# Experts of a routed feed-forward layer worked off by halves of 512 slots

## The reference, cut to what matters

```python
x = x + 0.5 * ffn(layernorm(x))     # first part
x = x + attention(layernorm(x))     # 16 heads, causal, with positions from a running sum
x = x + 0.5 * ffn(layernorm(x))     # second part, the same weights
```

```python
probs = softmax(xf @ gate_w.T)                   # [8192, 8]
scores_sel = route(probs)                        # 0 where a token isn't kept
h = gelu(einsum('nd,efd->enf', xf, w1))          # exact gelu
y_e = einsum('enf,edf->end', h, w2)
y = einsum('ne,end->nd', scores_sel, y_e)
```

## Time and profile before

| | |
|---|---|
| median of 3 runs | 2959.88 us (2959.29 to 2960.41) |
| profiled execution, its time | 2933.87 us |
| its span, first to last instruction | 2931.7 us |
| busy: PE / PEld / DVE / ACT / POOL | 84% / 65% / 58% / 57% / 34% of the span |
| instructions | 104032 |
| mean granted TensorE clock | 0.918 of full speed |
| DMA | 207.26 MB, mean 71 GB/s |

### The profile page before, as it was taken

How to read it: one execution, slowest core, us unless ns; L and a number is a source line. 1 busy time by engine, 2 the same in 40 slices (tenths; PEclk the granted TensorE clock), 3 DMA queues, 4 the chain that set the end, 5 groups by cost and what they waited for, 6 DMA issues and landing times. The chain is left out here.

```text
span 2931.7 us, 104032 instructions
## 1 busy us (share of the span) xinstructions
PE 2448.4 (84%) x45962; PEld 1906.9 (65%) x45964; DVE 1713.1 (58%) x3589; ACT 1674.4 (57%) x2102; POOL 990.4 (34%) x1423
## 2 busy tenths in 40 slices
PE   7287645577899999899999989999989999972875
PEld 4155412366688887778888768888778888741554
DVE  6733168888576568766566786666675111177331
ACT  6022123356677777667777767777766777560221
POOL 1078710244232224422222442322243222110787
PEclk9598866799999999999999999999999999985988
DMA  6455511121211112212112222111222111161555
GB/s 230 136 97 104 77 39 30 48 62 40 64 52 57 52 46 79 65 50 60 53 52 56 77 62 57 57 53 56 65 66 61 47 47 47 55 230 22 103 100 75
DMA packets 185107, 207.26 MB, mean 71 GB/s; under 512 B 35984, under 2 KB 151712, under 8 KB 184480
## 3 DMA queue, kind: packets, MB, share of 16 engines
q1 hardware_dynamic: 158880, 165.60, 19.0%
q0 software_dynamic: 24576, 34.10, 7.4%
q10 hardware_dynamic: 1152, 0.26, 0.0%
HBM read 131.68 MB, written 76.02 MB: 71 GB/s over the span
## 5 line engine op out<-in xcount | busy, mean ns | idle before, releaser
L1620 PEld LDWEIGHTS at_mix<-at_val,at_ew 128*64 128x64 f32 x34816 | 1223.5, 138 | 240.7 <-issue 36.1
L1204 ACT ACTIVATE at_ew<-at_ring 128x1024 f32<-128x1024 f32 (+1 forms) x1280 | 1125.2, 898 | 361.1 <-PE at_ring L1602 355.1
L1620 PE MATMUL at_mix<-at_val,at_ew 128*64 128x68 f32 x34816 | 1262.7, 224 | 45.0 <-DVE at_mixed L1466 30.1
L1602 PE MATMUL at_ring<-at_qT,at_kT 98*64 98x512 bf16 (+3 forms) x5120 | 698.7, 352 | 55.7 <-ACT at_ew L1204 36.2
L1125 POOL TENSOR_SCALAR_AFFINE_SELECT at_ew<-at_ew 128x256 f32<-128x256 f32 x512 | 292.6, 576 | 1078.2 <-ACT at_ew L1204 1077.2
L1466 DVE TENSOR_TENSOR at_mixed<-at_mix,at_prob 128x272 f32<-128x272 f32 x256 | 112.3, 439 | 437.1 <-PE at_mix L1620 435.7
L1602 PEld LDWEIGHTS at_ring<-at_qT,at_kT 98*64 98x64 bf16 x5120 | 228.7, 111 | 109.1 <-ACT at_ew L1204 48.3
L1147 POOL TENSOR_TENSOR at_val<-at_vo,at_val 128x256 f32<-128x256 f32 x384 | 266.6, 715 | 7.5
L328 POOL DMA_INDIRECT out_dram<-ffn_xn,ffn_idx_all x128 | 212.9, 1663 | 53.2 <-issue 34.1
L318 POOL DMA_INDIRECT ffn_xn<-table,ffn_idx_all x128 | 123.2, 963 | 311.8 <-DMA ffn_idx_all<-ffn_idx_hi 273.5
L1685 PE MATMUL at_side<-at_w_all,at_turned 128*64 128x512 f32 (+1 forms) x1024 | 203.2, 542 | 13.8 <-DVE at_bounded L1459 5.2
(11 more groups left out here) (224 smaller groups left out, 2759.8 us busy)
## 6 DMA issues: line engine op xcount, KB each, us to landing
table<-ffn_xn SPq DMA_DIRECT2D x32, 512.0 KB, 6.2
q_parts<-at_parts SPq DMA_DIRECT2D x64, 192.0 KB, 2.4
k_parts<-at_parts SPq DMA_DIRECT2D x64, 192.0 KB, 3.0
at_qT<-q_parts SPq DMA_DIRECT2D x128, 96.0 KB
at_kT<-k_parts SPq DMA_DIRECT2D x64, 192.0 KB
ffn_front<-in_L_attn_x_dram SPq DMA_DIRECT2D x16, 512.0 KB, 5.1
ffn_w_in<-in_L_ffn_w_dram SPq DMA_DIRECT2D x32, 256.0 KB, 3.6
at_xin<-out_dram SPq DMA_DIRECT2D x32, 256.0 KB, 5.9
```

Source lines behind the costliest of these rows:

```text
L1204: act.activation(ew[u % NE_BUF][:, a:b], ring[u % 2][:, a:b], ACT.Exp).then_inc(s["exp_ready"], 1)
L1602: lastm = pe.matmul(ring[u % 2][h:h + HALF, at:at + (CH - t) * P], kT[q][:, kc + j * P + h:kc + j * P + h + HALF], qT[q][:, qc + t * P:qc ...
L1620: m = pe.matmul(mix[block_of[u] % 2][h:h + HALF, t * K * VW:(t + 1) * K * VW], ew[u % NE_BUF][:, col + h:col + h + HALF], val[q][:, tile0 ...
```

## The change

TensorE's part of an expert is split by halves s of 512 slots: turn the rows of half 0, first layer of half 0, turn the rows of half 1, outputs of half 0, first layer of half 1, outputs of half 1. Before, it was both turns, both first layers, all outputs. ScalarE follows this order: copy and two GELUs for each half. The gathers are counted by halves: each buffer has two semaphores, of four DMAs each, and TensorE and VectorE wait for the half that they need. VectorE computes `slot_score` in two halves, with `picks` for expert e + 2 behind the first one.

Besides, the residual copy in the first part now counts to `rows_stored`, so that GpSimd waits for it ahead of gather(0) where it waited behind gather(1); and six semaphores of the first stage are merged into one counter for ScalarE (`act_stage`) and one for VectorE (`dve_stage`), each waited for at the same places as before.

```diff
-        gateT_ready = sem("gateT_ready")
+        act_stage = sem("act_stage")
+        dve_stage = sem("dve_stage")
         x_loaded = [sem(f"x_loaded{b}") for b in range(XB)]
+        GATE_TURNED, LOGITS_COPIED, EXPED = 1, 2, 3
+        SHIFTED, ORDER_READY, SCORE_READY = 1, 2, 3
...
         w_loaded = [sem(f"w_loaded{q}") for q in range(2)]
-        gathered = [sem(f"gathered{q}") for q in range(2)]
+        gathered = [[sem(f"gathered{q}_{s}") for s in range(2)] for q in range(2)]
...
                 if residual:
-                    sp.dma_start(dst, src).then_inc(residual_copied, 16)
+                    sp.dma_start(dst, src).then_inc(rows_stored, 16)
...
                         pool.wait_ge(turned_ps, (e - 1) * 3)
-                        pool.wait_ge(slot_score_ready, e - 1)
+                        pool.wait_ge(slot_score_ready, e * 2 - 2)
...
-                        ).then_inc(gathered[e % 2], 16)
+                        ).then_inc(gathered[e % 2][j // (J // 2)], 16)
...
-                pool.wait_ge(rows_stored, 16 * G + 16)
+                pool.wait_ge(rows_stored, 16 * G + (32 if residual else 16))
                 gather(0)
                 gather(1)
-                if residual:
-                    pool.wait_ge(residual_copied, 16)
...
@@ -398,9 +393,8 @@
                             act.wait_ge(h_ps, e * 4)
                         act.activation(xeT[:, :, s * 512:(s + 1) * 512], ring[1 + s][:, :, :],
                                        ACT.Copy).then_inc(turned, 1)
-                    if e >= 1:
-                        act.wait_ge(y_ps, e * J)
-                    for s in range(2):
+                        if s == 0 and e >= 1:
+                            act.wait_ge(y_ps, e * J)
                         for f in range(FK):
                             n = 2 * s + f
                             act.wait_ge(h_ps, e * 4 + n + 1)
...
                     q = e % 2
-                    dve.wait_ge(gathered[q], (e // 2 + 1) * 16 * J)
-                    dve.tensor_scalar(slot_score[q][:, :], rows[q][:, :, D + e], 0.5, None, ALU.mult
-                                      ).then_inc(slot_score_ready, 1)
-                    if e + 2 < NE:
-                        picks(e + 2)
-                        finish_picks(e + 2)
-                    dve.wait_ge(slot_score_ready, e + 1)
+                    halves = [slice(s * J // 2, (s + 1) * J // 2) for s in range(2)]
+                    for s in range(2):
+                        dve.wait_ge(gathered[q][s], (e // 2 + 1) * 16 * J // 2)
+                        dve.tensor_scalar(slot_score[q][:, halves[s]], rows[q][:, halves[s], D + e], 0.5, None, ALU.mult
+                                          ).then_inc(slot_score_ready, 1)
+                        if s == 0 and e + 2 < NE:
+                            picks(e + 2)
+                            finish_picks(e + 2)
+                    dve.wait_ge(slot_score_ready, e * 2 + 2)
                     if e >= 2:
                         dve.wait_ge(added, (e - 1) * J * 16)
...
-                    pe.wait_ge(gathered[q], (e // 2 + 1) * 16 * J)
-                    for s in range(2):
+                    def turn_rows(s):
+                        pe.wait_ge(gathered[q][s], (e // 2 + 1) * 16 * J // 2)
                         free(1 + s)
                         for t in range(J // 2):
                             for k in range(DK):
@@ -686,8 +682,7 @@
                                                     rows[q][:, s * (J // 2) + t, k * P:(k + 1) * P], ident[:, :])
                         last.then_inc(turned_ps, 1)
 
-                    pe.wait_ge(idx_hi_ready, min(e + 2, NE))
-                    for s in range(2):
+                    def hidden(s):
                         pe.wait_ge(turned, e * 3 + 2 + s)
                         for f in range(FK):
                             n = 2 * s + f
@@ -697,15 +692,24 @@
                                 last = pe.matmul(bank[n % 2][:, :], w1T[q][:, k, f * P:(f + 1) * P],
                                                  xeT[:, k, s * 512:(s + 1) * 512], start=(k == 0), stop=(k == DK - 1))
                             last.then_inc(h_ps, 1)
-                    for j in range(J):
-                        pe.wait_ge(h_ready, e * 4 + (2 if j < J // 2 else 4))
-                        if e >= 1 or j >= 2:
-                            pe.wait_ge(y_ready, e * J + j - 1)
-                        for f in range(FK):
-                            last = pe.matmul(bank[2 + j % 2][:, 0:D], hT[:, f, j * P:(j + 1) * P],
-                                             w2T[q][:, f, :], start=(f == 0), stop=(f == FK - 1))
-                        last.then_inc(y_ps, 1)
-
+
+                    def output(s):
+                        for j in range(s * J // 2, (s + 1) * J // 2):
+                            pe.wait_ge(h_ready, e * 4 + 2 * s + 2)
+                            if e >= 1 or j >= 2:
+                                pe.wait_ge(y_ready, e * J + j - 1)
+                            for f in range(FK):
+                                last = pe.matmul(bank[2 + j % 2][:, 0:D], hT[:, f, j * P:(j + 1) * P],
+                                                 w2T[q][:, f, :], start=(f == 0), stop=(f == FK - 1))
+                            last.then_inc(y_ps, 1)
+
+                    turn_rows(0)
+                    pe.wait_ge(idx_hi_ready, min(e + 2, NE))
+                    hidden(0)
+                    turn_rows(1)
+                    output(0)
+                    hidden(1)
+                    output(1)
 
                 for q in range(2):
                     slots(q)
```

More of the change, by code:

```diff
@@ L250, in _ @@
                     store(g)
-                sp.wait_ge(order_ready, 1)
+                sp.wait_ge(dve_stage, ORDER_READY)
                 for e in range(1, NE, 2):
@@ L455, in _ @@
                                   logit.rearrange("p t g e -> p e g t"),
[L456 to L457 removed]
+                                  row_g.unsqueeze(1).to_broadcast([P, NE, G, GT]), ALU.subtract).then_inc(dve_stage, 1)
+                dve.wait_ge(act_stage, EXPED)
                 ch(dve.tensor_reduce(row_t[:, :], by_t(prob), AX.X, ALU.add))
@@ L491, in _ @@
                                             op0=ALU.add, op1=ALU.add))
-                dve.tensor_tensor(order[:, :, :], order[:, :, :], work[:, :, :], ALU.min).then_inc(order_ready, 1)
+                dve.tensor_tensor(order[:, :, :], order[:, :, :], work[:, :, :], ALU.min).then_inc(dve_stage, 1)
                 dve.scalar_tensor_tensor(out=score[:, :, :].rearrange("p t e -> p e t"), in0=by_e(bank[3][:, :]),
                                          scalar=THRESHOLD, in1=prob[:, :, :], op0=ALU.is_lt,
-                                         op1=ALU.mult).then_inc(score_ready, 1)
+                                         op1=ALU.mult).then_inc(dve_stage, 1)
                 ch(dve.memset(low[:, :], NOT_CHOSEN))
@@ L598, in _ @@
                 last.then_inc(turns_ps, 1)
-                pe.wait_ge(gateT_ready, 1)
+                pe.wait_ge(act_stage, GATE_TURNED)
                 def turn(g):
@@ L624, in _ @@
                 logits(G - 1)
-                pe.wait_ge(logits_ready, 1)
+                pe.wait_ge(act_stage, LOGITS_COPIED)
                 for t in range(GT):
```

20 lines of the change are left out of this document (6 added, 14 removed).

## The result

| | before | after |
|---|---|---|
| median, same chip | 2960.14 us (2959.29 to 2962.59, 4 runs) | 2941.68 us (2932.58 to 2947.01, 4 runs) |
| profiled execution, its time | 2933.87 us | 2932.58 us |
| its span | 2931.7 us | 2930.5 us |
| first part's experts | 214.0 us | 211.9 us |
| second part's experts | 213.7 us | 213.2 us |

The ratio is 0.9937 (95%: 0.992 to 0.9955): 18.5 us faster. The forecast of 2946.7 had the direction, and its range, 2943 to 2952.5, missed the median by 1.3 us at the low end. But the two profiled executions are only 1.3 us apart. So the first question is which of the two speaks for the change.

What follows compares the result with a forecast made beforehand. GpSimd's gathers and scatters were taken to bound the expert stages. Start -9.75 and collisions -3.5 sum to -13.2 us, all else 0: from a timed median of 2959.88 to 2946.7 us, range 2943 to 2952.5.

Steps and rivals of the forecast that it cites:

- Merged counters and residual copy: Feed-forward parts: same waits at the same places, and the copy lands 27.7 us before GpSimd is released; cost 0.
- Start by halves: Expert 0, both parts: GpSimd's idle before the first scatter, 4.84 and 5.51 us, becomes 0.30; gain 9.75 us.
- the lower end of 7.9: Expert 0, both parts: the start's gain in us if TensorE's clock stays low after its first burst is split.
- Later experts 21.4 us of TensorE under GpSimd's 26.4: Later experts: 2.0 us of new waits bring TensorE to 21.4 us, under GpSimd's 26.4 to 26.6; cost 0.
- Rival E: Experts 1 to 7, both parts: new bubbles keep TensorE at 1.2 GHz and it becomes the bound; 3003 us, chance 0.02.
- Gather(2) hidden: Expert 2's indices land between 2744.5 and 2747.3, before GpSimd wants gather(2) at 2747.6; no cost, narrowly in the bad case.
- Fewer collisions: Experts 4 and 5, both parts: picks move beside gathers instead of scatters; gain 3.5 us, bounds gain 10 to loss 8.
- those 26 us: Whole kernel: the timed median before lies 26.0 us above the profiled execution; unexplained and carried unchanged into the forecast.
- A: Both expert stages: the forecast itself, earlier start plus fewer collisions, 2946.7 us; chance 0.65.
- B: Both expert stages: start gain only, picks move but collide as often because phases differ; -9.75, 2950.1 us, chance 0.2.
- C: Expert 0: TensorE stays at 1.2 GHz, start and gather(2) come later, no fewer collisions; about -5, 2955 us, chance 0.06.
- D: Expert 0: the first four gathers land only with the last four, gaining 2.2 us per part; 2955.5 us, chance 0.05.

Runs made afterwards that it cites:

- after_again: The changed kernel, unedited, measured a second time against the kernel before on one chip: ratio 0.9952 (0.9938 to 0.9965), 2923.24 us.
- first_expert_only: The changed kernel with the halves' order on TensorE and ScalarE for expert 0 alone, against the kernel before: 0.9945 (0.9932 to 0.9958), 2919.69 us.

## Why the prediction was right and where it failed

- **Merged counters and residual copy, forecast 0.** Right: 0.9992, 0.9998 and 1.0001, against 1.0003 for no change at all. The one 0.9983 did not repeat.
- **Start by halves, forecast -9.75.** Right in four of five profiles of the kernel after. That it is right to the hundredth says little: both gaps fell to GpSimd's usual 0.30 us and were counted from the profile that the forecast used; against the seven profiles without halves the term is 9.0 to 9.75. On the way there: landing 2.80 us in the first profile and 3.13 in the second (2.89 reckoned), ScalarE's bubble 1.21 (1.2), first output ready 2728.35 - 2710.31 = 18.0 us after the first gather (17.5 reckoned). Half the first layer took 5.42 us: the clock was low until 2724.0, 6.7 us after the first turn and not 5.5. The first output was ready 2.65 us ahead of need, so the later clock cost nothing, and the lower end of 7.9 did not come. The Trainium skill's "TensorE: Matmul & The Clock Gate" (Part 1) says that the clock is set by how busy the engine has lately been; the broken burst rose to 2.4 GHz 1.2 us later than the unbroken one had, which agrees with it, only the size was too small to reach GpSimd.
- **Later experts 21.4 us of TensorE under GpSimd's 26.4.** Right: 2738.28 to 2759.52 is 21.24 us. Rival E, with low clock there, is excluded by a granted clock of 0.89 and 0.90 in the stages. By the section "A second HAM failure mode: psum-queue depth-cycling" of the Trainium skill's "TensorE: Matmul & The Clock Gate" it would have been likelier. No expert here showed such swinging: from 2725 to 2800 us of after_again, with bubbles of 1.26 and 0.69 us in each 21.2 us, the granted clock was 1.00 throughout.
- **Gather(2) hidden.** Right: no gap before it; expert 0's outputs and its slot matmuls were over at 2740.35.
- **Fewer collisions, forecast -3.5.** This term was mis-sized: it measured -1.1 against the profile that the forecast used, and -0.7 against the mean of seven without the halves. The places were right within 1 us: 2740.8, 2762.0, 2783.3 and 2807.8 for 2741, 2763, 2784.2 and 2807.4. The prices were not. I took the mean of 1.3 us for the six runs that meet scatters; by the instructions over 1.55 us they cost 0.9 in expert 1, 1.7 in expert 2 and 1.9 in expert 3, the mean is 1.5. I took 0.4 for the four beside gathers; three cost 0.5 to 0.8, the fourth nothing. The step should have been priced by phase, that is by how long after the begin of `picks` a transfer starts. The scatter of expert 1 started 1.5 us behind it, in the second operation, those of experts 2 and 3 started 0.7 and 0.5 us behind it, in the first, and all three end 0.17 to 0.23 us behind the end of VectorE's third operation (2762.73 + 3.06 = 2765.79 against 2764.38 + 1.23 = 2765.61). In the kernel before, six of the ten runs had a scatter that started 0.07 to 0.28 us behind the begin and ended some 0.33 us behind the end of the second operation already, after 2.4 to 2.6 us. So a shift of a few tenths of a us lengthened that scatter by 0.5 to 0.9 us, of which the next one gave back 0.3 (1.74 for 2.05), though the forecast's "in scatter(1), as before" is right. That the moved `picks` helps is shown, at 2.2 us.
- **The total and its range.** Over four comparisons the change gave 0.9952, 0.995, 0.9958 and 0.996, that is 14.6, 13.8, 12.9 and 12.0 us of medians, and the forecast was 13.2. That the mean of these four, 13.3, is so near is partly luck: the stages show only 10.5, since the collision term was too large, and some 3 us more lie in the medians which no stage in a trace holds. In the first comparison it was 18.5; its interval (0.992 to 0.9955) contains the first two of the four ratios and not the other two. The step of the prediction that failed is the one that carried the sum over to the median: "I cannot place those 26 us and leave them as they are". The offset did not stay. Before, the timed runs lay 26 us above the profiled one; after, three lie 8 to 14 us above, although the profiled one had the late outputs in it, and it counts among the four. Without it the median is 2942.96, at the edge of the range. In the fifteen runs that followed, the profiled execution lay between 6.3 us below and 5.6 us above the median of its own run, so a profiled execution is not 26 us faster as such. The range took in only the bounds of the terms and nothing of the scatter of single executions, 14.4 us among those four. Why that first comparison lay 20 us above all later ones for the kernel before, and whether its 4 to 6.5 us of additional gain are chance or belong to it, stays open: no trace of its unprofiled runs exists.
- **The rivals.** A's start held and its collisions did not. By the stages (-10.5 to -10.8) B, start only with -9.75, is nearer than A's -13.2, while the four ratios leave room for both. B's reason, that the phases differ from those drawn, was right in the small: the places were as drawn within 1 us, and tenths of a us within them decided the price. C and D are excluded by gaps of 0.30 and landings of 2.80 and 3.13 us; D's "under half busy" holds for the eighth gather and not for the fourth (0.96 and 0.53 in the two windows of 2 us from 2714 of the kernel before), and the halves landed apart all the same. The late outputs of the first profile were in no rival.

## What to carry to other kernels

When a serial queue (here GpSimd's transfers) bounds a stage, shortening the way to its first item pays the idle gap before it, here down to the usual 0.30 us. Splitting the work behind it further costs cover; the shortest stages here came from splitting the first round alone (415.1 us against 417.2, one profile of each on the same chip; the intervals of their times overlap). Price collisions between engines by the phase at which one starts within the other, not by a mean, and expect a change at the start to shift that phase for all that follows. And for a gain below 1%, compare stages of the trace, which repeat within a few us here, put the scatter of whole executions into the range, and repeat a comparison before an edit that should be nothing is believed to be something.

## What the runs showed of the hardware that was not expected

**Late outputs.** In one of five profiled executions of the kernel after, in both parts, VectorE started on the first output 5.1 and 5.3 us behind TensorE's first output instruction, against 1.2 us in all eight other profiled executions that have expert 0 by halves. The granted clock was full when these instructions ran and fell only while TensorE stood. ScalarE's copy of the second half, which waits for the turns just ahead of the outputs, was late too, by 0.6 and 0.9 us (in the second part 2727.53, with the turns over at 2726.67; in after_again 2726.85 and 2726.82), so the delay begins before the outputs. It made 5.9 us of gaps before the fifth scatters and 3.3 before the first. No cause was found; whether it belongs to one execution or to the first comparison's chip, which is not on record, is open too.

**GpSimd's transfers beside VectorE's bf16 operations.** A scatter of 1.55 us took up to 3.46 us in the kernel before and up to 3.83 in the kernel after, a gather of 0.95 up to 2.65 in first_expert_only, while VectorE's operations kept their 1.2 us. Three cases: a scatter that starts just ahead of `picks` and one that starts inside it, in after_again, second part, and the longest one, in the first profile after:

```profile
2740.42 1.55 POOL L325 DMA_INDIRECT out_dram<-ffn_xn,ffn_idx_all  x1 [0.30 <-issue]
2740.78 1.21 DVE L550 TENSOR_TENSOR ffn_front<-ffn_digits,ffn_hi 128x2048 bf16<-128x2048 bf16 x1
...
2783.27 1.21 DVE L550 TENSOR_TENSOR ffn_front<-ffn_digits,ffn_hi 128x2048 bf16<-128x2048 bf16 x1
2785.65 1.23 DVE L552 TENSOR_TENSOR ffn_front<-ffn_front,ffn_count_b 128x2048 bf16<-128x2048 bf16 x1
```

```profile
2846.79 3.83 POOL L325 DMA_INDIRECT out_dram<-ffn_xn,ffn_idx_all  x1 [0.30 <-issue]
2849.22 1.22 DVE L552 TENSOR_TENSOR ffn_front<-ffn_front,ffn_count_b 128x2048 bf16<-128x2048 bf16 x1
```

In the second case the scatter is the one of 3.29 us from 2783.82, shown further up; it ends at 2787.11, 0.23 us behind the third operation. In all seventeen profiles, with one exception, a scatter that starts 0.5 to 2.0 us behind the begin of `picks` ends 0.16 to 0.24 us behind the end of the third operation. One that starts 0.04 to 0.4 us behind it ends 0.30 to 0.36 us behind the end of the second; the exceptions are four that started at 0.31 and ran on to the third (3.46 us). The gathers keep a distance as well, another one: those that start in the first operation and take over 1.04 us end 0.80 to 0.83 us behind the end of an operation (2808.19 + 1.64 = 2809.83, against 2807.80 + 1.22 = 2809.02).

The Trainium skill's "SBUF — State Buffer" ("SBUF: two separate sides") says that VectorE and GpSimd share a port pair which one of them holds for a whole instruction while the other blocks. Ends at a fixed distance behind the end of a VectorE operation agree with that. The first case does not: the scatter from 2740.42 and VectorE's operation from 2740.78 ran beside each other, and neither took longer than alone. So the lock as described isn't all of it.
